# Windowed attention and a mixture of experts on eight cores: two software-pipelined steps of the attention loop are issued further behind their producer

## The chip, the cores and the metric

The kernel runs as one program on all 8 cores of a Trainium2 chip (two dies of four cores). Each core works on its own 2048 tokens and no core waits for another. The metric is the device time in microseconds (us) of the slowest core.

## What is computed

One layer on x of shape (2, 8192, 1024): attention over a window of 17 positions with 16 heads of 64, then a feed-forward part with 8 experts (the best two of each token are weighted) and a shared expert. Each part is followed by a residual addition and a layer normalization. The change concerns the first part, cut to its core here:

```python
q = _ln(silu(x @ Wq).reshape(B, L, H, D), q_g, q_b)
k = _ln(kv[..., :C].reshape(B, L, H, D), k_g, k_b).reshape(B, L, C)
scores = stack([einsum('blhd,blhd->blh', q, k_pad[:, w:w + L]) for w in range(K)]) * SCALE
attn = softmax(scores - (1.0 - soft_mask) * MASK_PENALTY, axis=-1)
out = sum(attn[..., w][..., None] * v_pad[:, w:w + L] for w in range(K))
x = _layernorm(x + silu(out @ Wout))
```

## The kernel before

A core takes its tokens in two halves of 1024, one after the other. A half goes through these stages: transposing x, the projections to q, k, v; the attention loop; normalization and router; the shared expert and four pairs of experts; the last normalization.

`Prog` (from line 70) records all operations in program order and gives each engine its own, in that order. It adds semaphore waits where two operations touch the same bytes (in PSUM: the same bank). So every engine runs strictly in the order in which the Python code emits, and an instruction that waits holds back all behind it on its engine. DMAs are issued by the queue of an engine (`sync` here), and wait in that queue's order too. The helpers give the profile its line numbers: matmuls are L336 (`mm`), transposes on TensorE L342 (`tr`), activations L351 (`act`), copies on ScalarE L355 (`scopy`), VectorE's operations L363 and L364 (`vop`), DMAs L328.

The attention loop (line 716) runs over 8 tiles of 128 tokens. A round i does, in this order:

- `knorm(i + 2)` and `qnorm(i + 1)`: two VectorE operations each, from `kpark` and `qpark` into `bscr`, for k also 8 transposes and a copy into R2.
- The scores of tile i: 8 transposes of q, a VectorE operation into `qfm`, then 32 matmuls, 144 columns for each head, into the banks of `ps_A` and `ps_B`. ScalarE copies them to `swide`, and SP stores them to `scdram` in two DMAs.
- `emit_W(i - 3)` from round 3 on: the output projection. Two products of 8 matmuls of 512 columns, each followed by a tanh on ScalarE and two VectorE operations on `fscr`; both products use the same bank, `wob[i % 2]`. Then the residual addition into `xtm` on VectorE and a square with a sum on ScalarE.
- `emit_B(i - 2)` from round 2 on: attention times v. SP reads the weights of 144 columns for each head back from `awdram` into a buffer of `awideP`; 32 transposes, four copies by ScalarE, 32 matmuls of 64 columns, two copies, 8 more transposes and a last copy into `qpark`.
- `emit_A(i)`: SP gathers the 17 scores of each position out of `scdram` into `ccg`; VectorE and ScalarE compute the softmax (the exponential is ScalarE's operation on `ccg`), the result is `abfc`, and SP scatters it along the diagonals to `awdram`.

W(i) needs B(i) and B(i) needs A(i). After the loop stand the B's and W's that are left, in the order B(6), W(5), B(7), W(6), W(7), which I call the tail. Behind it stand the sums of the layer normalization (`u1st`), which need all 8 W's. `awideP` (line 614) has two buffers before the change, one in R1, which is free after the projections, and one in the first 2304 columns of `kpark`, whose k tiles 0 to 2 have been normalized by round 0.

Of the kernel before, what the change touches and what calls it, by code (L numbers as in the profile page):

```python
# [18 lines left out]
NT = 8  # L19
# [12 lines left out]
WIDE = NH * 144  # L32
# [186 lines left out]
def build_program():  # L219
# [34 lines left out]
    with contextlib.ExitStack() as st:  # L254
        def sb(name, shape, dt):
            return st.enter_context(nc.sbuf_tensor(name, shape, dt))
# [14 lines left out]
        R1 = sb("R1", [128, 9216], BF16)  # L271
# [3 lines left out]
        kpark = sb("kpark", [128, 9216], BF16)  # L275
# [37 lines left out]
        awideP = None  # L313
# [13 lines left out]
        def dma(eng, dst, src, tag=""):  # L327
            P.op(eng, lambda e, d=dst, s=src: e.dma_start(out=d, in_=s),  # L328
                 rd=[src], wr=[dst], dma=True, tag=tag)
# [24 lines left out]
        def scopy(out, in_, tag=""):  # L354
            P.op("scalar", lambda e, o=out, i=in_: e.copy(o, i),  # L355
                 rd=[in_], wr=[out], tag=tag)
# [67 lines left out]
        for half in range(_HLIM):  # L424
          try:
# [185 lines left out]
                    abfc[i % 3][:].rearrange("p (h w) -> p h w", h=NH),  # L611
                    tag=f"asc{hx}")

            awideP = [R1[:, 6144:6144 + WIDE], kpark[:, 0:WIDE]]

            wob = [ps_A[:, 1024:1536], ps_B[:, 1024:1536]]

            def emit_W(i):
                ao_fm = qpark[:, 1024 * i:1024 * (i + 1)]
                pg = wob[i % 2]  # L620
                th = fscr[i % 2]
                for gi in range(2):
                    for c in range(8):
                        mm(pg, ao_fm[:, 128 * c:128 * c + 128],
                           WOUT[:, 1024 * c + 512 * gi:1024 * c + 512 * gi + 512],
                           c == 0, c == 7, tag=f"wo{hx}")
                    act(th[:, 512 * gi:512 * gi + 512], pg, AF.Tanh, scale=0.5,
                        tag=f"woth{hx}")
                    vop("tensor_scalar", th[:, 512 * gi:512 * gi + 512],
                        [th[:, 512 * gi:512 * gi + 512], 0.5, 0.5],  # L630
                        (ALU.mult, ALU.add), tag=f"wosg{hx}")
                    vop("tensor_tensor", th[:, 512 * gi:512 * gi + 512],
                        [th[:, 512 * gi:512 * gi + 512], pg], (ALU.mult,),
                        tag=f"wosl{hx}")
                xsl = xtm[:, 1024 * i:1024 * (i + 1)]
                vop("scalar_tensor_tensor", xsl, [th[:], 1.0, xsl],
                    (ALU.bypass, ALU.add), accum=u1st[:, i:i + 1], tag=f"u1{hx}")
                act(qfm[0][:], xsl, AF.Square, accum=u1st[:, NT + i:NT + i + 1],
                    tag=f"u1sq{hx}")

            def emit_B(i):
                aw = awideP[i % 2]
                dma("sync", aw, aw_dram[i], tag=f"awrb{hx}")
                ao_tm = R1[:, 4096 + 1024 * (i % 2):4096 + 1024 * (i % 2) + 1024]
                for w in range(2):
                    for hh in range(8):
                        s = 8 * w + hh
                        tr(ps_t0[:, 128 * hh:128 * hh + 128],
                           aw[:, 144 * s:144 * s + 128], tag=f"aT{hx}")
                        tr(ps_t1[0:16, 128 * hh:128 * hh + 128],  # L650
                           aw[:, 144 * s + 128:144 * s + 144], tag=f"aTb{hx}")
                    scopy(ATa[w], ps_t0[:], tag=f"aTe{hx}")
                    scopy(ATb[w], ps_t1[0:16, :], tag=f"aTbe{hx}")
                    av = (ps_A[:, 0:512], ps_A[:, 512:1024])[w]
                    for hh in range(8):
                        s = 8 * w + hh
                        mm(av[:, 64 * hh:64 * hh + 64],
                           ATa[w][:, 128 * hh:128 * hh + 128],
                           R3[:, 1024 * i + 64 * s:1024 * i + 64 * s + 64],
                           True, False, tag=f"av{hx}")  # L660
                        mm(av[:, 64 * hh:64 * hh + 64],
                           ATb[w][0:16, 128 * hh:128 * hh + 128],
                           R3[0:16, 1024 * (i + 1) + 64 * s:
                              1024 * (i + 1) + 64 * s + 64],
                           False, True, tag=f"avb{hx}")
                    scopy(ao_tm[:, 512 * w:512 * w + 512], av, tag=f"aoev{hx}")
                for c in range(8):
                    tr(ps_t0[:, 128 * c:128 * c + 128],
                       ao_tm[:, 128 * c:128 * c + 128], tag=f"aoT{hx}")
                scopy(qpark[:, 1024 * i:1024 * (i + 1)], ps_t0[:],  # L670
                      tag=f"aofm{hx}")
# [44 lines left out]
            for i in range(NT):  # L716
                if i + 2 <= NT:
                    knorm(i + 2)
                if i + 1 < NT:
                    qnorm(i + 1)  # L720
                qt = bscr[i % 2]
                pst = (ps_t0, ps_t1)[i % 2]
                for c in range(8):
                    tr(pst[:, 128 * c:128 * c + 128], qt[:, 128 * c:128 * c + 128],
                       tag=f"qT{hx}")
                vop("tensor_scalar", qfm[i % 2][:], [pst[:], gq_c, qbS_c],
                    (ALU.mult, ALU.add), tag=f"qfme{hx}")

                if _S3 < 2:
                    continue  # L730
                for s in [x for x in range(NH) if x % 2 == 0] + \
                         [x for x in range(NH) if x % 2 == 1]:
                    if s < 9:
                        dst = ps_A[:, 512 * (s // 3) + 144 * (s % 3):
                                   512 * (s // 3) + 144 * (s % 3) + 144]
                    else:
                        j = s - 9
                        dst = ps_B[:, 512 * (j // 3) + 144 * (j % 3):
                                   512 * (j // 3) + 144 * (j % 3) + 144]
                    lhs = qfm[i % 2][64 * (s % 2):64 * (s % 2) + 64,  # L740
                                     128 * (s // 2):128 * (s // 2) + 128]
                    rhs = R2[64 * (s % 2):64 * (s % 2) + 64,
                             1152 * (s // 2) + 128 * i:1152 * (s // 2) + 128 * i + 144]
                    mm(dst, lhs, rhs, True, False, tag=f"sc{hx}")
                    rhsb = bmask[64 * (s % 2):64 * (s % 2) + 64,
                                 128 * i:128 * i + 144]
                    mm(dst, lhs, rhsb, False, True, tag=f"scb{hx}")
                if _S3 < 3:
                    continue
                fs_sw = swide[:].ap[0][0]  # L750
                srcA = bass.AP(ps_A[:].tensor, int(ps_A[:].offset),
                               [[1536, 128], [512, 3], [144, 3], [1, 144]])
                dstA = bass.AP(swide[:].tensor, 0, [[fs_sw, 128], [432, 3],
                                                    [144, 3], [1, 144]])
                scopy(dstA, srcA, tag=f"scevA{hx}")
                dma("sync", bass.AP(sc_dram[i].tensor, 0,
                                    [[2304, 128], [1, 1296]]),
                    swide[:, 0:1296], tag=f"scoutA{hx}")
                srcB1 = bass.AP(ps_B[:].tensor, int(ps_B[:].offset),
                                [[1536, 128], [512, 2], [144, 3], [1, 144]])  # L760
                dstB1 = bass.AP(swide[:].tensor, 1296, [[fs_sw, 128], [432, 2],
                                                        [144, 3], [1, 144]])
                scopy(dstB1, srcB1, tag=f"scevB{hx}")
                srcB2 = bass.AP(ps_B[:].tensor, int(ps_B[:].offset) + 1024,
                                [[1536, 128], [1, 144]])
                scopy(swide[:, 2160:2304], srcB2, tag=f"scevB2{hx}")
                dma("sync", bass.AP(sc_dram[i].tensor, 1296,
                                     [[2304, 128], [1, 1008]]),
                    swide[:, 1296:2304], tag=f"scoutB{hx}")
                if i >= 3:  # L770
                    emit_W(i - 3)
                if i >= 2:
                    emit_B(i - 2)
                emit_A(i)
            emit_B(NT - 2)
            emit_W(NT - 3)
            emit_B(NT - 1)
            emit_W(NT - 2)
            emit_W(NT - 1)

            ck(7)
            table(AF.Ln, AF.Exp)
# [334 lines left out]
```

How the kernel before makes its waits and increments, by code:

```python
            def _run(eng):  # L179
                for o in ops:
                    if o.eng != eng_name:
                        continue
                    need = {}
                    for d in o.deps:
                        p = ops[d]
                        pc = chan(p)
                        if not need_edge(p, o):
                            continue
                        m = p if p.inc else p.marker
                        assert m is not None, f"no marker for op {p.i} ({p.tag})"
                        v = m.cnt
                        if need.get(pc, 0) < v:
                            need[pc] = v
                    if o.dma and o.prev_target > 0:
                        if need.get(o.slot, 0) < o.prev_target:
                            need[o.slot] = o.prev_target
                    for pc in sorted(need):
                        v = need[pc]
                        if floors.get(pc, 0) >= v:
                            continue
                        eng.wait_ge(sems[pc], v)
                        floors[pc] = v
                    ins = o.emit(eng)
                    if o.inc:
                        ins.then_inc(sems[chan(o)], 16 if o.dma else 1)
                if eng_name == "sync":
                    for c in sorted(totals):
                        if c != "sync" and floors.get(c, 0) < totals[c]:
                            eng.wait_ge(sems[c], totals[c])
```

## Time and profile before

| what | value |
| --- | --- |
| time, median of 2 runs | 2311.78 us (2304.62 to 2318.95) |
| the profiled execution, its own time | 2316.63 us |
| its span, slowest core (0) | 2315.0 us |
| spans of the 8 cores | 2282.0 to 2315.0 us |
| TensorE (PE) busy, matmuls | 1564.6 us, 68% |
| VectorE (DVE) busy | 577.5 us, 25% |
| ScalarE (ACT) busy | 563.2 us, 24% |
| GpSimd (POOL) busy | 117.7 us, 5% |
| granted TensorE clock, core 0, mean | 0.773 of 2.4 GHz |

The span is the time from the first to the last instruction of a core in the profile; the profiled execution's own time lies 1.6 us above it. A row of the timeline gives the start and the duration in us, the engine, the line, the operation and its tiles (output <- input), and in brackets how long the engine had been idle and what ended that. "SPq" is SP's DMA queue, and its rows are issues and not transfers. Buffer numbers are left out in the names, so `R` stands for R1, R2 and R3 and `awdram` for all eight of its kind. The granted clock is a share of 2.4 GHz; 0.50 is 1.2 GHz.

### The profile page before, as it was taken

What the parts mean: (1) busy time and instruction counts of PE and PEld (TensorE: products, weight loads), DVE (VectorE), ACT (ScalarE), POOL (GpSimd) and SP (SyncE); (2) the same over time, 40 slices, a digit from 0 to 9 for tenths busy, and PEclk for the clock granted to TensorE, in tenths of its full rate; (3) what the DMA queues carried; (4) which work ended last, traced back from release to release, by engine and by line L of the source; (5) the groups of instructions that cost most, each with busy time, mean ns of one, the idle gap of its engine ahead of it and who ended that gap; (6) DMA issues with size and microseconds to landing.
All of it is one profiled execution on the core that took longest, in us unless ns stands there. A gap on an engine that the chain in (4) does not pass through costs nothing.

```text
span 2315.0 us, 22914 instructions; the slowest of 8 cores (2282.0 to 2315.0 us)
## 1 busy us (share of the span) xinstructions
PE 1564.6 (68%) x8368; PEld 793.4 (34%) x8492; DVE 577.5 (25%) x878; ACT 563.2 (24%) x834; POOL 117.7 (5%) x136
## 2 busy tenths in 40 slices
PE   0594255656466989889816932556564779899895
PEld 0342133323333434344403422333324334344442
DVE  0154222211311222212212542222113122212223
ACT  0353132222321112021203531222223212121122
POOL 0120000000200000000001200000002000000000
PEclk9997555556588989999956965555565889999998
DMA  9222211220182525540292222121202624445203
GB/s 227 46 37 48 70 35 50 53 45 12 19 127 37 73 37 74 78 68 1 37 203 57 37 57 60 36 65 38 56 0 43 104 37 73 67 79 73 37 1 109
DMA packets 142342, 139.38 MB, mean 60 GB/s; under 512 B 73239, under 2 KB 106136, under 8 KB 142234
## 3 DMA queue, kind: packets, MB, share of 16 engines
q0 software_dynamic: 60960, 84.55, 23.6%
q1 hardware_dynamic: 76890, 36.60, 6.4%
q10 hardware_dynamic: 4384, 16.78, 2.2%
q8 instruction: 70, 1.15, 0.2%
q14 instruction: 38, 0.31, 0.0%
HBM read 189.36 MB, written 33.10 MB: 96 GB/s over the span
## 4 chain that ended last, share of the span: by engine, by line
PE 61%; DMA 15%; DVE 9%; ACT 7%; issue 6%; another core or an unknown queue 2%; SPq 0%; DVEq 0%; ACTq 0%; POOL 0%; POOLq 0%
PE ps_A L336 37%; PE ps_B L336 16%; PE ps_t L342 8%; DVE bscr L364 3%; ACT R L355 3%; DMA wpool<-Su 3%; DMA qpark<-Wd 2%; DMA wpool<-Wd 2%; DMA scdram<-swide 2%; DMA wpool<-Sd 1%; DMA wrf<-Wr 1%; DVE xtm L364 1%; DVE fscr L364 1%; DMA bscr<-x 1%
## 5 line engine op out<-in xcount | busy, mean ns | idle before, releaser
L336 PE MATMUL ps_A<-wpool,R 128*128 128x512 bf16 x2118 | 497.8, 386 | 36.6 <-DMA wpool<-Su 18.3
L342 PE MATMUL ps_t<-sb_ident,bscr 128*128 128x128 bf16 x1312 | 147.0, 264 | 340.6 <-DVE bscr L364 208.5
L355 ACT COPY R<-ps_t 128x512 bf16<-128x512 bf16 (+2 forms) x242 | 186.4, 784 | 670.6 <-PE ps_t L342 667.6
L336 PEld LDWEIGHTS ps_A<-wpool,R 128*128 128x128 bf16 x2176 | 210.9, 99 | 279.8 <-issue 53.8
L336 PE MATMUL ps_B<-wpool,R 128*128 128x512 bf16 (+1 forms) x1072 | 238.4, 368 | 41.9 <-DMA wpool<-Sd 25.9
L351 ACT ACTIVATE fscr<-ps_A 128x512 f32<-128x512 f32 x228 | 136.8, 600 | 487.6 <-PE ps_A L336 472.7
L342 PEld LDWEIGHTS ps_t<-sb_ident,bscr 128*128 128x128 bf16 x1312 | 112.8, 118 | 394.2 <-issue 361.7
L336 PE MATMUL ps_A<-qpark,R 128*128 128x512 bf16 x750 | 179.5, 383 | 3.9 <-DVE xtm L364 2.9
L336 PEld LDWEIGHTS ps_B<-wpool,R 128*128 128x128 bf16 x1088 | 101.4, 100 | 167.3 <-issue 59.5
L336 PE MATMUL ps_A<-R 128*128 128x64 bf16 (+1 forms) x512 | 86.6, 228 | 75.9 <-ACT R L355 75.9
L342 PE MATMUL ps_t<-sb_ident,R 128*128 128x128 bf16 (+1 forms) x384 | 72.1, 282 | 46.2 <-DMA R<-awdram 41.6
L336 PEld LDWEIGHTS ps_A<-qpark,R 128*128 128x128 bf16 x768 | 73.3, 99 | 84.3 <-issue 10.2
L364 DVE SCALAR_TENSOR_TENSOR bscr<-ps_B,rwall,fscr 128x512 bf16<-128x512 f32 x64 | 48.1, 751 | 198.9 <-PE ps_A L336 175.1
L364 DVE SCALAR_TENSOR_TENSOR bscr<-ps_A,rwall,fscr 128x512 bf16<-128x512 f32 x64 | 48.1, 751 | 189.2 <-PE ps_A L336 189.2
L336 PEld LDWEIGHTS ps_A<-R 128*128 128x128 bf16 (+1 forms) x512 | 52.1, 102 | 111.8 <-issue 84.1
L336 PE MATMUL ps_B<-qpark,R 128*128 128x512 bf16 x252 | 69.9, 433 | 16.1 <-DMA qpark<-Wd 15.9
L364 DVE SCALAR_TENSOR_TENSOR xtm<-ps_B,xtm 128x512 f32<-128x512 f32 x64 | 41.3, 687 | 152.9 <-PE ps_B L336 152.9
L364 DVE TENSOR_SCALAR fscr<-fscr 128x512 f32<-128x512 f32 x32 | 13.7, 427 | 253.4 <-ACT fscr L351 253.4
L336 PE MATMUL ps_B<-wpool,qpark 128*128 128x512 bf16 x122 | 48.8, 569 | 30.5 <-DVE fscr L364 22.6
L342 PEld LDWEIGHTS ps_t<-sb_ident,R 128*128 128x128 bf16 (+1 forms) x384 | 35.5, 106 | 81.0 <-issue 53.9
L364 POOL CAST bscr<-xtm 128x1024 bf16<-128x1024 f32 x16 | 18.4, 1155 | 844.5 <-DVE xtm L364 792.0
L336 PE MATMUL ps_A<-sb_validrow,sb_bkrow 1*128 1x512 f32 (+1 forms) x12 | 8.7, 825 | 77.0 <-DMA sb_validrow<-validrow 63.9
(136 smaller groups left out, 1419.8 us busy)
## 6 DMA issues: line engine op xcount, KB each, us to landing
scdram<-swide SPq DMA_DIRECT2D x16, 648.0 KB, 3.0
xtm<-x ACTq DMA_DIRECT2D x2, 4096.0 KB, 30.5
wpool<-Wkv POOLq DMA_DIRECT2D x4, 2048.0 KB, 34.1
qpark<-Wg POOLq DMA_DIRECT2D x8, 1024.0 KB, 29.2
kpark<-Wu POOLq DMA_DIRECT2D x8, 1024.0 KB, 33.8
wpool<-Wg POOLq DMA_DIRECT2D x8, 1024.0 KB, 15.5
wpool<-Wu POOLq DMA_DIRECT2D x8, 1024.0 KB, 21.1
qpark<-Wd POOLq DMA_DIRECT2D x8, 1024.0 KB, 10.1
```

The costliest lines, as they stand in the source:

```text
L336: e.matmul(d, l, r, start=s0, stop=s1),
L342: P.op("tensor", lambda e, d=dst, s=src: e.transpose(d, s, ident[:]), rd=[src, ident[:]], wr=[dst], tag=tag, strips=strips)
L351: e.activation(o, i, f, bias=b, scale=s, accum_out=a),
L355: P.op("scalar", lambda e, o=out, i=in_: e.copy(o, i), rd=[in_], wr=[out], tag=tag)
L364: return f(o, *ii, *aa)
```

## The change

`emit_B` is issued three rounds behind `emit_A` of its tile and no longer two, `emit_W` five rounds behind and no longer three, and within a round W stands ahead of B as before. `awideP` gets a third buffer, columns 2304 to 4607 of `kpark` (k tiles 2 to 4, all normalized by round 2; the buffer is first written in round 5). After the loop there are now three B's and then five W's. No operation is added or taken away.

```diff
-            awideP = [R1[:, 6144:6144 + WIDE], kpark[:, 0:WIDE]]
+            awideP = [R1[:, 6144:6144 + WIDE], kpark[:, 0:WIDE],
+                      kpark[:, WIDE:2 * WIDE]]
...
             def emit_B(i):
-                aw = awideP[i % 2]
+                aw = awideP[i % 3]
                 dma("sync", aw, aw_dram[i], tag=f"awrb{hx}")
...
+                if i >= 5:
+                    emit_W(i - 5)
                 if i >= 3:
-                    emit_W(i - 3)
-                if i >= 2:
-                    emit_B(i - 2)
+                    emit_B(i - 3)
                 emit_A(i)
-            emit_B(NT - 2)
-            emit_W(NT - 3)
-            emit_B(NT - 1)
-            emit_W(NT - 2)
-            emit_W(NT - 1)
+            for i in range(NT - 3, NT):
+                emit_B(i)
+            for i in range(NT - 5, NT):
+                emit_W(i)
```

What this moves, at three places of the first half. On ScalarE in round 2, from the last copy of the scores (`swide<-ps_B`) on; the copies `R<-ps_t` up to `qpark<-ps_t` are B(0), `ccg<-ccg` is the exponential of A(2). Before:

```order
L355 COPY swide<-ps_B 128x144
L355 COPY R<-ps_t 128x1024
L355 COPY R<-ps_t 16x1024
L355 CAST R<-ps_A 128x512
L355 COPY R<-ps_t 128x1024
L355 COPY R<-ps_t 16x1024
L355 CAST R<-ps_A 128x512
L355 COPY qpark<-ps_t 128x1024
L351 ACTIVATE ccg<-ccg 128x272
L351 ACTIVATE R<-ps_t,gb 128x8x128
```

And after, at the same place:

```order
L355 COPY swide<-ps_B 128x144
L351 ACTIVATE ccg<-ccg 128x272
L351 ACTIVATE R<-ps_t,gb 128x8x128
L355 COPY swide<-ps_A 128x1296
L355 COPY swide<-ps_B 128x864
L355 COPY swide<-ps_B 128x144
L355 COPY R<-ps_t 128x1024
```

The seven operations of B(0) have left round 2 and stand behind the scores of round 3.

On ScalarE at the end of the tail, from the last copy of B(7) to the loading of the next activation table; `fscr` x2 are the two tanh of a W, `qfm,u1st` its square. Before:

```order
L355 COPY qpark<-ps_t 128x1024
L351 ACTIVATE fscr<-ps_A 128x512 x2
L351 ACTIVATE qfm,u1st<-xtm 128x1024
L351 ACTIVATE fscr<-ps_B 128x512 x2
L351 ACTIVATE qfm,u1st<-xtm 128x1024
L385 ACT_TABLE_LOAD
```

And after:

```order
L355 COPY qpark<-ps_t 128x1024
L351 ACTIVATE fscr<-ps_B 128x512 x2
L351 ACTIVATE qfm,u1st<-xtm 128x1024
L351 ACTIVATE fscr<-ps_A 128x512 x2
L351 ACTIVATE qfm,u1st<-xtm 128x1024
L351 ACTIVATE fscr<-ps_B 128x512 x2
L351 ACTIVATE qfm,u1st<-xtm 128x1024
L351 ACTIVATE fscr<-ps_A 128x512 x2
L351 ACTIVATE qfm,u1st<-xtm 128x1024
L351 ACTIVATE fscr<-ps_B 128x512 x2
L351 ACTIVATE qfm,u1st<-xtm 128x1024
L385 ACT_TABLE_LOAD
```

Five W's follow each other where two did; W(5), which stood between B(6) and B(7), is among them, and W(3) and W(4) come out of rounds 6 and 7.

On SP's queue from the last score store (round 7) on. Before:

```order
L328 DMA scdram<-swide 128x1008
L328 DMA kpark<-awdram 128x2304
L328 DMA ccg<-scdram 128x16x17
L328 DMA awdram<-abfc 128x16x17
L328 DMA R<-awdram 128x2304
L328 DMA kpark<-awdram 128x2304
```

And after:

```order
L328 DMA scdram<-swide 128x1008
L328 DMA kpark<-awdram 128x2304
L328 DMA ccg<-scdram 128x16x17
L328 DMA awdram<-abfc 128x16x17
L328 DMA kpark<-awdram 128x2304
L328 DMA R<-awdram 128x2304
L328 DMA kpark<-awdram 128x2304
```

Behind the last scatter (`awdram<-abfc`) three reads for B's stand instead of two.

## Rows read from the trace of the kernel before

**Rows 1.** The page's chain that ended last, shares of the span.

```profile
PE 61%; DMA 15%; DVE 9%; ACT 7%; issue 6%; another core or an unknown queue 2%; SPq 0%; DVEq 0%; ACTq 0%; POOL 0%; POOLq 0%
```

**Rows 2.** Waits in 205 to 590 us: total us, times, longest.

```profile
DVE sm L364 <- ACT ccg L351: 93.5, 8, 15.4
```

**Rows 3.** Timeline of ScalarE: the exponentials of rounds 1 and 2.

```profile
264.09 0.43 ACT L351 ACTIVATE ccg<-ccg 128x272 f32<-128x272 f32 x1 [10.09 <-DVE ccg L364]
...
303.60 0.43 ACT L351 ACTIVATE ccg<-ccg 128x272 f32<-128x272 f32 x1
```

**Rows 4.** Timeline of SP's queue, first half: score stores of rounds 1 to 5.

```profile
253.11 3.48 SPq L328 DMA_DIRECT2D scdram<-swide  x2
...
277.03 3.41 SPq L328 DMA_DIRECT2D scdram<-swide  x2
...
316.55 3.48 SPq L328 DMA_DIRECT2D scdram<-swide  x2
...
357.32 3.80 SPq L328 DMA_DIRECT2D scdram<-swide  x2
...
400.47 3.77 SPq L328 DMA_DIRECT2D scdram<-swide  x2
```

**Rows 5.** The same of the second half, rounds 1 to 5.

```profile
1406.70 3.42 SPq L328 DMA_DIRECT2D scdram<-swide  x2
...
1432.83 3.39 SPq L328 DMA_DIRECT2D scdram<-swide  x2
...
1472.35 3.71 SPq L328 DMA_DIRECT2D scdram<-swide  x2
...
1513.49 3.44 SPq L328 DMA_DIRECT2D scdram<-swide  x2
...
1555.56 3.46 SPq L328 DMA_DIRECT2D scdram<-swide  x2
```

**Rows 6.** Chain in order of time: reads for B(0) and B(3).

```profile
280.70 4.41 DMA R<-awdram
...
404.39 5.81 DMA kpark<-awdram
```

**Rows 7.** Timeline of TensorE: B(6) and W(7)'s second product; second half B(6).

```profile
522.06 1.11 PE L342 MATMUL ps_t<-sb_ident,R 128*128 128x128 bf16 x5 [13.66 <-DMA R<-awdram]
...
579.56 1.01 PE L336 MATMUL ps_B<-wpool,qpark 128*128 128x512 bf16 x2 [4.82 <-DVE fscr L364]
...
1670.81 1.32 PE L342 MATMUL ps_t<-sb_ident,R 128*128 128x128 bf16 x6 [10.99 <-DMA R<-awdram]
```

**Rows 8.** Timeline of ScalarE: B(6)'s last copy, tanhs of W(5), W(6), W(7).

```profile
539.28 1.01 ACT L355 COPY qpark<-ps_t 128x1024 bf16<-128x1024 bf16 x1 [0.82 <-PE ps_t L342]
542.40 0.60 ACT L351 ACTIVATE fscr<-ps_B 128x512 f32<-128x512 f32 x1 [2.10 <-PE ps_B L336]
...
569.06 0.60 ACT L351 ACTIVATE fscr<-ps_A 128x512 f32<-128x512 f32 x1 [2.13 <-PE ps_A L336]
573.11 0.60 ACT L351 ACTIVATE fscr<-ps_A 128x512 f32<-128x512 f32 x1 [3.45 <-PE ps_A L336]
...
577.52 0.58 ACT L351 ACTIVATE fscr<-ps_B 128x512 f32<-128x512 f32 x1
583.14 0.60 ACT L351 ACTIVATE fscr<-ps_B 128x512 f32<-128x512 f32 x1 [5.05 <-PE ps_B L336]
```

**Rows 9.** Timeline of VectorE: W(7)'s residual addition, first and second half.

```profile
585.16 1.23 DVE L363 SCALAR_TENSOR_TENSOR xtm<-fscr,xtm 128x1024 f32<-128x1024 f32 x1
...
1734.80 1.23 DVE L363 SCALAR_TENSOR_TENSOR xtm<-fscr,xtm 128x1024 f32<-128x1024 f32 x1
```

**Rows 10.** Stretches: us, busy times PE, PEld, DVE, ACT, POOL; clock, DMA, GB/s.

```profile
571.00:575.00 4.00, 3.61 (x16) 1.49 (x16) 1.08 (x2) 0.60 (x1) 0.00 (x0) 1.00 0.02 4
...
580.00:583.00 3.00, 3.00 (x8) 0.85 (x6) 0.00 (x0) 0.00 (x0) 0.00 (x0) 0.53 0.00 0
```

## The prediction

> **What bounds the kernel now.** I read the chain that ended last first [rows 1]: TensorE holds 61% of it, and in the attention stage the rest is handed between engines and DMA. So I looked there, in each half from the first scores (about 225 us) to the end of the output projections (586 us), for what a round of the loop waits on. In that stretch VectorE waits 93.5 us in eight waits for ScalarE's exponential of `ccg` [rows 2]: the softmax of a round. ScalarE works in program order, and the timeline shows what stands ahead of that exponential. In round 1, where no B is issued, it starts at 264.09 and ends an idle time of 10.09 us that VectorE's `ccg` set. In round 2, after B(0), it starts at 303.60 without idle time, behind B's last copy [rows 3]. What follows it (reciprocal, `abfc`, knorm, qnorm, transposes, the next scores) is therefore late by B. A round with B costs what B costs; B is not beside other work.
>
> The length of a round is the distance between the SP queue's issues of score stores (`scdram<-swide`). First half: 253.11, 277.03, 316.55, 357.32, 400.47, so round 1 takes 23.92 (no B, no W), round 2 39.52 (B alone), round 3 40.77, round 4 43.15 (W and B) [rows 4]. Second half: 26.13, 39.52, 41.14, 42.07 [rows 5]. So B costs 13.4 to 15.6 us in a round, but a W beside it only 1.3 to 3.6: W stands ahead of B on TensorE, in the time in which B's input is still on its way. Without W that wait shows: the read of `awdram` takes 4.41 us in round 2, and 5.81 into kpark in round 5 [rows 6].
>
> **The change part by part.** The third buffer costs and frees nothing: before, a read is issued right behind the score stores (280.70 in round 2 [rows 6]), so no read waited for its buffer. SP's order in a round stays: score stores, read for B, gather, scatter. What counts is where the B's and W's now stand.
>
> Loop. B(0) leaves round 2, which becomes a round like round 1: first half 39.52 - 23.92 = 15.6 saved, second 39.52 - 26.13 = 13.4, together 29.0 [rows 4, 5]. Rounds 3 and 4 keep a B (an earlier one) and lose their W. Round 3 becomes like round 2: 40.77 - 39.52 and 41.14 - 39.52, 2.9 saved. Round 4's B reads into kpark, where I add the 5.81 - 4.41 = 1.4 of the longer landing [rows 6]: 40.92, so 2.2 and 1.2 saved, 3.4. The bounds for rounds 3 and 4 are 0 (the wait takes all that W leaves) and 9.1 (both at 39.52, no longer landing). Rounds 5 to 7 have one W and one B as before, of lower numbers but of the same banks (W(i-5) has the parity of W(i-3)), and cost the same. Loop, both halves: 29.0 + 2.9 + 3.4 = 35.3 saved.
>
> Tail. Behind the loop stood B W B W W and stands B B B W W W W W. The first B still waits for its read, which SP issues behind the last scatter: 13.66 and 10.99 us of idle TensorE [rows 7]. That doesn't change, for B(5)'s read stands behind the same scatter, and the reads for B(6) and B(7) land behind an earlier B. From the first transpose of the first B to the end of the last residual addition, before: 585.16 + 1.23 - 522.06 = 64.3 in the first half, 1734.80 + 1.23 - 1670.81 = 65.2 in the second [rows 7, 9].
>
> After, with durations of the first half. One B, from its first transpose to the end of its last copy: 539.28 + 1.01 - 522.06 = 18.2, and the next B's transposes need the bank which that copy reads, so 18.3 from B to B. Two such steps, 36.6. The third B up to the first tanh of the W behind it: 542.40 - 522.06 = 20.3 [rows 7, 8]. Then the W's. In a row they don't overlap much. Both halves of one W use one PSUM bank, and the first tanh of the next W stands on ScalarE behind the square of this one: W(6)'s first tanh is at 569.06, its second at 573.11, W(7)'s first at 577.52. That is 8.46 from W to W [rows 8]. It was W(6) at the high clock: in 571 to 575 the granted clock was 1.00 (2.4 GHz). W(7)'s second product came after 4.82 us of idle TensorE, and in 580 to 583 the clock was 0.53, mostly the low level of 1.2 GHz [rows 7, 10]. W(7)'s second tanh, at 583.14, comes 5.6 behind its first, where W(6)'s came 4.05 behind: 1.6 for the slow product [rows 8]. A W in a row thus takes 8.46 with the clock high and 8.46 + 1.6 = 10.1 with it low; both levels stand within these few us, so for the three in the middle I take the mean, 9.3. First W 8.46, three of 9.3, and the last one from its first tanh to the end of its addition 586.39 - 577.52 = 8.9. The W's: 8.5 + 27.9 + 8.9 = 45.3. Tail after: 36.6 + 20.3 + 45.3 = 102.2, that is 37.9 more in the first half and 37.0 in the second, 74.9 together.
>
> Sum: 74.9 - 35.3 = 39.6 us slower. The profiled execution took 2316.6 us (span 2315.0), so it would be 2356.2; the median of the runs is 4.8 us below that execution, so 2311.8 + 39.6 = 2351.4. What stands behind the tail (normalization, router, the FFN with its weights) moves as a whole: its first weight loads are issued on GpSimd behind casts that need the last W.
>
> Bounds of the terms: W's all at the high clock, 2 x (3 x 0.84 + 1.6) = 8.2 less; all at the low one, 2 x (3 x 0.8 + 1.6) = 8.0 more. Rounds 3 and 4: 2.8 less or 6.3 more. Altogether +29 to +54.
>
> On the clock the Trainium skill ("TensorE: Matmul & The Clock Gate", section "HAM oscillation — how this bites in real kernels") states a rule that speaks against this change: idle gaps between bursts of matmuls put the array back to half clock, so that each burst begins slow. The trace agrees for the one gap of this kind, W(7)'s of 4.82 us. By the rule all W's in a row would go slow, which is the first rival below; by the mean of the two rows the sum stays as above.
>
> **The rivals.** First, the W's in a row all run slow. Five W's with TensorE idle twice in each let the clock fall every time: 10.1 a piece, 8.0 us above the sum, 2359.4. For it: the gap and the slow product of W(7). Against: W(7)'s first product ran right behind W(6)'s second, at the high clock [rows 10], and in a row each W but the first has such a start.
> Second, they all run at the high clock: 8.2 below, 2343.2. For it W(6); against it W(7).
> Third, on the other side: the W's overlap. They alternate between two banks and two `fscr` buffers, so five in a row might run at the distance from one's second tanh to the next's first, 577.52 - 573.11 = 4.41 us [rows 8], with the first part hidden. Tail then 36.6 + 20.3 + 4 x 4.41 + 8.9 = 83.4, 19.1 and 18.2 more, 37.3 - 35.3 = +2.0: 2313.8, no slower. It decides if ScalarE can take W(7)'s first tanh before W(6)'s square. The order says no, and in the trace that tanh starts at 577.52 right behind it.
> A gain is left only if B's in a row cost much less than 18.3, or if the kpark read's wait vanished in rounds that I hold unchanged; no row speaks for it.
>
> **How the numbers follow.** Forecast 0.60, first rival 0.20, second 0.15, third 0.03, anything else 0.02. A measurement of this kernel tells about 2% from no change, 46 us here, so the line lies at 2358.0. The forecast is 6.6 us under it: of its 0.60 I give 0.08 to slower, of the first rival 0.15. Faster 0.02, within 2% 0.75, slower 0.23. Range 2335 to 2364: it takes in both clock rivals with some us of spread of the runs (2304.6 to 2319.0), and leaves out the overlap.
>
> **What would show it.** Right: score stores of rounds 2 and 3 some 24 to 26 us apart (was 39.5), rounds 3 and 4 at 39.5 to 41, rounds 5 to 7 unchanged, the idle time of 11 to 14 us before the first B of the tail still there, B's 18.3 apart, first tanhs of W's 8.5 to 10.1 apart, and the residual additions ending about 102 us behind that B's first transpose. Wrong: a tail under 90 us, a round 2 that keeps 39 us, or a read of `awdram` for which B(6) or B(7) waits.

## The result and the profile after

The changed kernel takes 2354.37 us (median of 11 runs; before 2312.19, median of 10). The ratio to the kernel before is 1.0191, with a 95% interval of 1.016 to 1.0222, so 44 us slower (37 to 51). The forecast was 2351.4 us, 39.6 us slower. A second measurement on another chip gave 1.0174 (1.013 to 1.0217), 40 us.

The execution profiled with the result was disturbed on both dies, so the rows are those of the same kernel's second profile (the run `again` below; slowest core 2367.5 us, time 2369.1, 8 cores from 2338.1 to 2367.5; the kernel before spanned 2282.0 to 2315.0). They are from its core 1.

The timeline of SP's queue, score stores of rounds 1 to 5 in the first half (start and duration in us), answers to [rows 4]:

```profile
257.62 3.50 SPq L328 DMA_DIRECT2D scdram<-swide  x2
...
281.32 3.54 SPq L328 DMA_DIRECT2D scdram<-swide  x2
...
305.16 4.35 SPq L328 DMA_DIRECT2D scdram<-swide  x2
...
345.63 3.65 SPq L328 DMA_DIRECT2D scdram<-swide  x2
...
385.32 3.47 SPq L328 DMA_DIRECT2D scdram<-swide  x2
```

Rounds 1 to 4 take 23.70, 23.84, 40.47 and 39.69 us, where they took 23.92, 39.52, 40.77 and 43.15. Round 2 has become a round like round 1, and rounds 3 and 4 cost what a B alone costs (39.52 in round 2 before).

Then the tail. TensorE waits for the read of B(5) as it waited for B(6)'s [rows 7]; ScalarE's last copies of B(5), B(6), B(7) and the tanhs of W(3) to W(5) answer to [rows 8], VectorE's last residual addition to [rows 9]:

```profile
506.39 3.46 PE L342 MATMUL ps_t<-sb_ident,kpark 128*128 128x128 bf16 x16 [14.74 <-DMA kpark<-awdram]
```

```profile
523.63 1.01 ACT L355 COPY qpark<-ps_t 128x1024 bf16<-128x1024 bf16 x1 [0.82 <-PE ps_t L342]
...
542.02 1.01 ACT L355 COPY qpark<-ps_t 128x1024 bf16<-128x1024 bf16 x1 [0.82 <-PE ps_t L342]
...
560.42 1.01 ACT L355 COPY qpark<-ps_t 128x1024 bf16<-128x1024 bf16 x1 [0.82 <-PE ps_t L342]
...
563.84 0.60 ACT L351 ACTIVATE fscr<-ps_B 128x512 f32<-128x512 f32 x1 [2.40 <-PE ps_B L336]
569.57 0.60 ACT L351 ACTIVATE fscr<-ps_B 128x512 f32<-128x512 f32 x1 [5.13 <-PE ps_B L336]
572.92 1.06 ACT L351 ACTIVATE qfm<-xtm 128x1024 bf16<-128x1024 f32 x1 [2.75 <-DVE xtm L363]
573.89 0.19 ACT L351 ACTIVATION_READ_ACCUMULATOR qfm<-xtm 128x1 f32 x1
573.98 0.58 ACT L351 ACTIVATE fscr<-ps_A 128x512 f32<-128x512 f32 x1
579.32 0.60 ACT L351 ACTIVATE fscr<-ps_A 128x512 f32<-128x512 f32 x1 [4.76 <-PE ps_A L336]
...
583.73 0.58 ACT L351 ACTIVATE fscr<-ps_B 128x512 f32<-128x512 f32 x1
```

```profile
611.84 1.23 DVE L363 SCALAR_TENSOR_TENSOR xtm<-fscr,xtm 128x1024 f32<-128x1024 f32 x1
```

B's stand 18.4 us apart (523.63, 542.02, 560.42). The tail runs from 506.39 to 613.07, 106.7 us, where 102.2 was forecast. What is longer are the W's: 563.84, 573.98, 583.73, 593.72, 603.83. They are 9.8 to 10.1 us apart and not 8.5 and 9.3. From W(4) on each first tanh follows the square and its sum directly, and each second tanh waits some 5 us for a slow product.

The clock of two neighbouring stretches of this row of W's, TensorE idle in the first and in W(5)'s second product in the other (columns as in [rows 10]):

```profile
581.40:585.40 4.00, 0.00 (x0) 0.00 (x0) 2.06 (x4) 1.63 (x3) 0.00 (x0) 1.00 0.00 0
585.60:589.20 3.60, 3.43 (x9) 1.26 (x10) 0.03 (x1) 0.00 (x0) 0.00 (x0) 0.54 0.00 0
```

The high level (1.00, 2.4 GHz) lies in the idle time, and the product gets mostly the low one (0.54, near 1.2 GHz). On this core W(6) and W(7) repeat it: 1.00 in the idle times, 0.50 and 0.52 in the second products. On all 8 cores and in both halves the second products of W(4) to W(7), 64 in all, take 2.85 to 3.57 us, and none the 1.89 of a product with the clock high throughout.

Since single cores differ, the experiments are compared by the mean over the 8 cores of each profile, read from the same rows of each core. A round is the distance between its score store and the next round's; the tail here is counted from round 7's score store to the end of the last residual addition, so it holds round 7's own B and the wait for the read. Both halves are summed, in us:

| kernel | round 1 | round 2 | round 3 | round 4 | rounds 5+6 | tail |
| --- | --- | --- | --- | --- | --- | --- |
| before | 49.8 | 80.3 | 81.7 | 84.2 | 155.8 | 209.4 |
| buf | 51.6 | 81.5 | 82.8 | 85.1 | 155.8 | 213.8 |
| again (the change) | 50.4 | 50.2 | 81.4 | 79.9 | 156.5 | 295.2 |
| w_only | 50.5 | 80.0 | 80.7 | 79.8 | 156.0 | 259.0 |
| b_only | 50.2 | 50.3 | 81.1 | 82.6 | 154.4 | 270.4 |
| late_sq | 49.8 | 49.7 | 80.7 | 80.2 | 156.4 | 270.2 |
| tail_mix | 50.6 | 50.9 | 81.3 | 79.6 | 156.4 | 282.4 |
| early_read | 49.8 | 80.4 | 82.5 | 83.9 | 155.6 | 188.0 |
| a_first | 50.5 | 72.3 | 75.0 | 74.7 | 145.4 | 188.8 |
| deep_a_first | 50.0 | 49.9 | 74.6 | 69.9 | 144.2 | 269.4 |
| lag1 | 74.1 | 73.0 | 77.6 | 73.0 | 145.1 | 136.6 |
| lag1_sq | 73.9 | 72.7 | 77.7 | 73.1 | 144.2 | 131.7 |

`before` and `buf` do the same work in the same order and show how far two profiles differ: 4.4 us in the tail, 1 to 2 in a round. Their mean is the base below: 80.9, 82.3, 84.7, 155.8, 211.6 for round 2, 3, 4, 5+6 and the tail.

### The profile page after: what moved, and what is told of

Read it like the earlier page. It is cut to its first block, busy times and chain, and to the rows that moved or that the text cites. A ratio compares the mean times of both kernels' runs of the same rounds, so it can differ in the third digit from the quotient of the medians.

```text
span 2412.7 us, 22932 instructions; the slowest of 8 cores (2339.6 to 2412.7 us)
## 1 busy us (share of the span) xinstructions
PE 1619.1 (67%) x8372; PEld 807.7 (33%) x8492; DVE 577.7 (24%) x878; ACT 563.1 (23%) x834; POOL 117.7 (5%) x136
## 4 chain that ended last, share of the span: by engine, by line
PE 60%; DMA 16%; DVE 9%; ACT 6%; issue 6%; another core or an unknown queue 2%; DVEq 0%; SPq 0%; ACTq 0%; POOL 0%; POOLq 0%
PE ps_A L336 37%; PE ps_B L336 15%; PE ps_t L342 8%; DVE bscr L364 3%; DMA wpool<-Su 2%; ACT R L355 2%; DMA scdram<-swide 2%; DMA qpark<-Wd 2%; DMA wpool<-Wd 2%; DMA wrf<-Wr 2%; DMA kpark<-awdram 1%; DVE fscr L364 1%; DMA bscr<-x 1%; DMA wpool<-Sd 1%
## 5 line engine op out<-in xcount | busy, mean ns | idle before, releaser
L336 PE MATMUL ps_A<-wpool,R 128*128 128x512 bf16 x2118 | 521.3, 399 | 35.9 <-DMA wpool<-Su 17.3
L336 PEld LDWEIGHTS ps_A<-wpool,R 128*128 128x128 bf16 x2176 | 216.5, 102 | 295.2 <-issue 120.0
L336 PE MATMUL ps_B<-wpool,R 128*128 128x512 bf16 (+1 forms) x1072 | 251.4, 383 | 39.7 <-DMA wpool<-Sd 25.4
L336 PE MATMUL ps_A<-qpark,R 128*128 128x512 bf16 x750 | 188.4, 397 | 4.0 <-DVE xtm L364 2.9
L342 PE MATMUL ps_t<-sb_ident,kpark 128*128 128x128 bf16 x320 | 67.4, 275 | 46.8 <-DMA kpark<-awdram 44.3
L364 DVE TENSOR_SCALAR fscr<-fscr 128x512 f32<-128x512 f32 x32 | 13.7, 427 | 269.4 <-ACT fscr L351 269.4
L342 PE MATMUL ps_t<-sb_ident,R 128*128 128x128 bf16 x320 | 60.3, 289 | 25.6 <-DMA R<-awdram 18.5
L336 PE MATMUL ps_A<-wpool,qpark 128*128 128x512 bf16 x122 | 46.5, 546 | 30.6 <-DVE fscr L364 26.8
L336 PE MATMUL ps_B<-wpool,qpark 128*128 128x512 bf16 x124 | 46.3, 539 | 30.7 <-DVE fscr L364 26.6
L336 PE MATMUL ps_A<-sb_validrow,sb_bkrow 1*128 1x512 f32 (+1 forms) x12 | 8.7, 825 | 82.3 <-DMA sb_validrow<-validrow 68.0
```

Source lines behind the costliest of these rows:

```text
L336: e.matmul(d, l, r, start=s0, stop=s1),
L342: P.op("tensor", lambda e, d=dst, s=src: e.transpose(d, s, ident[:]), rd=[src, ident[:]], wr=[dst], tag=tag, strips=strips)
L364: return f(o, *ii, *aa)
```

## The experiments

**The changed kernel again** (`again`), for a profile.

> The changed kernel once more, for a profile. Theory (sum of two tails against three rounds): 39.6 us over the kernel before; round 2 of the loop about 24 us long in the first half and 26 in the second, tail 102 us from the first B's first transpose to the last residual addition. Rival (the W's in a row all at the low clock): tail 106 us, 47 us over the kernel before. Rival (the W's overlap): tail 83 us, 2 us over.

1.0174 (1.013 to 1.0217), 40 us slower. Against the base the change takes 30.7 us off round 2, 0.9 off round 3 and 4.8 off round 4, and adds 83.6 to the tail: 47.9 with rounds 5+6, inside both timed intervals. The tail of core 1's first half, 106.7 us, is that of the first rival (106), while the timed loss lies nearer to the theory's. Over all cores and both halves, 64 distances between W's in a row average 9.91 us (8.46 to 10.15). The overlap is ruled out.

**The buffer alone** (`buf`): the order of before, three buffers.

```diff
-            awideP = [R1[:, 6144:6144 + WIDE], kpark[:, 0:WIDE]]
+            awideP = [R1[:, 6144:6144 + WIDE], kpark[:, 0:WIDE],
+                      kpark[:, WIDE:2 * WIDE]]
...
-                aw = awideP[i % 2]
+                aw = awideP[i % 3]
```

> Only the third buffer for the reads of awdram, order of before. Theory: no read waits for its buffer, so no change (within 3 us). Rival (the reads into the new columns of kpark land later, or meet the normalization's reads of kpark): slower by up to 1.4 us for each of the four reads that move there, 3 to 6 us.

1.0007 (0.9972 to 1.0042): no change. The buffer neither costs nor frees anything.

**The W's alone** (`w_only`):

```diff
-                if i >= 3:
-                    emit_W(i - 3)
+                if i >= 5:
+                    emit_W(i - 5)
                 if i >= 2:
                     emit_B(i - 2)
...
-            emit_B(NT - 2)
-            emit_W(NT - 3)
-            emit_B(NT - 1)
-            emit_W(NT - 2)
-            emit_W(NT - 1)
+            for i in range(NT - 2, NT):
+                emit_B(i)
+            for i in range(NT - 5, NT):
+                emit_W(i)
```

> Only the W's moved: B two rounds behind, W five, tail B B W W W W W. Theory: rounds 3 and 4 lose the W that stood in B's wait for its read and get 6 us shorter in all, the tail grows by 38 us (18.3 + 20.3 + 45.3 = 83.9 against 64.3 and 65.2), so 32 us slower than before, most of the whole loss. Rival (it is the B's that cost, since a B in a row costs what a round gained): within 5 us of before.

1.0145 (1.0106 to 1.0184), 34 us slower. Rounds 3 and 4 give 1.6 and 4.9, together the 6 expected, and the tail takes 47.4 where 38 were expected: again W's in a row (9.97 us apart on average). Most of the loss is made by the W's.

Why a round gains so little without its W can be seen on TensorE, where the B of round 3 begins (core 1, first half). In the kernel before, behind W(0):

```profile
326.50 2.77 PE L342 MATMUL ps_t<-sb_ident,kpark 128*128 128x128 bf16 x16 [1.00 <-DMA kpark<-awdram]
```

and here, where W(0) is gone:

```profile
326.07 3.46 PE L342 MATMUL ps_t<-sb_ident,kpark 128*128 128x128 bf16 x16 [8.68 <-DMA kpark<-awdram]
```

B starts at nearly the same time. The W had filled the wait for B's read, and without it TensorE stands idle there for 8.68 us.

**The B's alone** (`b_only`), each W one round behind its B as before:

```diff
-                if i >= 3:
-                    emit_W(i - 3)
-                if i >= 2:
-                    emit_B(i - 2)
+                if i >= 4:
+                    emit_W(i - 4)
+                if i >= 3:
+                    emit_B(i - 3)
                 emit_A(i)
+            emit_B(NT - 3)
+            emit_W(NT - 4)
             emit_B(NT - 2)
```

> B three rounds behind, W four (one behind B as before), two buffers, tail B W B W B W W. Theory: round 2 gives back 29.0 us and round 3 2.9 in both halves together; the tail grows by one B and one W between B's, 26.6 us in each half (from B(6)'s last copy to B(7)'s in the kernel before), 53.3; so 21 us slower than before. Rival (a B costs the same in the loop and behind it and the W's that go with it are free): within 5 us of before.

1.0071 (1.0039 to 1.0104), 16 us slower (21 expected). Round 2 gives 30.6, and the tail grows by 58.8 (53.3 expected). A B moved out of the loop together with a W is no gain either.

**The squares later** (`late_sq`, `late_sq2`): the changed kernel, with each W's square in the tail issued behind the next W's first tanh.

```diff
                     act(th[:, 512 * gi:512 * gi + 512], pg, AF.Tanh, scale=0.5,
                         tag=f"woth{hx}")
+                    if late and gi == 0 and i > NT - 5:
+                        sq_W(i - 1)
...
-                act(qfm[0][:], xsl, AF.Square, accum=u1st[:, NT + i:NT + i + 1],
-                    tag=f"u1sq{hx}")
+                if not late or i == NT - 1:
+                    sq_W(i)
```

> The changed kernel, with the square of each W in the tail issued behind the first tanh of the next W. Theory (ScalarE's order sets 4.41 us of the distance between two W's in a row, the slow product 5.7): the next first tanh starts when its product is done, some 3.5 us behind the second tanh at the low clock, so W's 9.2 us apart instead of 10.1 and about 7 us less than the changed kernel in the two tails together, 35 us over the kernel before. Rival (VectorE's residual addition sets the distance): W's stay at 10.1 and the time at 40 to 44 us over.

The tails are 25.0 us shorter than those of the changed kernel, more than three times the 7 expected; timed 1.0125 (1.0031 to 1.022). The timeline of ScalarE, core 1, W(4)'s second tanh, then both of W(5) and of W(6):

```profile
576.93 0.60 ACT L351 ACTIVATE fscr<-ps_B 128x512 f32<-128x512 f32 x1 [1.13 <-PE ps_B L336]
...
581.72 0.60 ACT L351 ACTIVATE fscr<-ps_B 128x512 f32<-128x512 f32 x1 [2.02 <-PE ps_B L336]
583.45 0.60 ACT L351 ACTIVATE fscr<-ps_A 128x512 f32<-128x512 f32 x1 [1.13 <-PE ps_A L336]
...
588.24 0.60 ACT L351 ACTIVATE fscr<-ps_A 128x512 f32<-128x512 f32 x1 [2.02 <-PE ps_A L336]
589.97 0.60 ACT L351 ACTIVATE fscr<-ps_B 128x512 f32<-128x512 f32 x1 [1.13 <-PE ps_B L336]
```

Here the first tanh of the next W comes 1.73 us behind the second of this one (581.72 to 583.45), not 4.41, and the second 4.79 behind the first, so W's stand 6.52 apart. The stretch behind these rows (same columns):

```profile
576.00:590.00 14.00, 8.06 (x36) 3.17 (x34) 7.61 (x14) 4.72 (x9) 0.00 (x0) 1.00 0.00 1
```

The clock is high throughout this stretch. TensorE's timeline shows how long it stood idle ahead of a second product, in this kernel

```profile
579.74 1.89 PE L336 MATMUL ps_B<-wpool,qpark 128*128 128x512 bf16 x8 [2.90 <-ACT qfm L351]
...
586.26 1.89 PE L336 MATMUL ps_A<-wpool,qpark 128*128 128x512 bf16 x8 [2.91 <-ACT qfm L351]
...
592.77 3.19 PE L336 MATMUL ps_B<-wpool,qpark 128*128 128x512 bf16 x8 [2.90 <-ACT qfm L351]
```

and in the changed one:

```profile
585.77 3.44 PE L336 MATMUL ps_B<-wpool,qpark 128*128 128x512 bf16 x8 [4.83 <-DVE fscr L364]
```

The earlier tanh was forecast; that with it the idle time falls from 4.8 to 2.9 us, and that most second products then run fast, was not in the expectation. Not all do: the third row, W(7)'s, has the same idle time ahead of it and is slow. Of the 64 second products of W(4) to W(7) on all cores 40 take 1.89 us here and 24 over 3 us, where none took less than 2.85 in the changed kernel. Over all cores the distance between W's is 7.00 us (5.77 to 8.46). That the shorter idle time is what keeps the clock high is likely but not shown, since no run changes it by itself. A second run of the same kernel (`late_sq2`) shows whether the time agrees:

> late_sq once more, since its first timing had an interval of 1.0 to 2.2% over before while the tails in its profile were 25 us shorter than those of the changed kernel. Theory: 18 us over the kernel before (43 - 25), W's in a row 6.5 us apart with a second product at the high clock. Rival (7 us less than the changed kernel, as expected at first, and the clock rose by chance): 35 us over, W's 9.2 apart on most cores.

1.0102 (1.0063 to 1.0141), 24 us over the kernel before: some 18 us less than the change, and the rival's 35 lies outside. On cores 4 to 7 of its profile W's stand 7.16 us apart on average (5.78 to 8.70): nearer to the 6.5 of the theory than to the rival's 9.2, with some second products still slow.

**Another order in the tail** (`tail_mix`): the changed kernel's loop, and behind it

```diff
             for i in range(NT - 3, NT):
                 emit_B(i)
-            for i in range(NT - 5, NT):
+                emit_W(i - 2)
+            for i in range(NT - 2, NT):
                 emit_W(i)
```

> The loop of the changed kernel, tail B W B W B W W W. Theory: a W between two B's costs 26.6 - 18.3 = 8.3 us instead of 10.1 in a row, for its sums run beside B's transposes, and three W's stand so: 5 us less in each half, 10 in all, 32 to 34 us over the kernel before. Rival (order in the tail is no matter, only how many B's and W's stand there): 40 to 44 us over.

The tails are 12.8 us shorter than those of the changed kernel (10 expected). The timing, 1.0188 (1.014 to 1.0236), doesn't show it; an interval of 22 us can't tell 10. So the profile speaks for it and the time leaves it open.

**B(6)'s read ahead of the last scatter** (`early_read`), in the kernel before; `load_B` is the read split off `emit_B`:

```diff
                 if i >= 2:
+                    load_B(i - 2)
                     emit_B(i - 2)
+                if i == NT - 1:
+                    load_B(NT - 2)
                 emit_A(i)
```

> The kernel before, with the read of awdram for B(6) issued ahead of emit_A(7) instead of behind its scatter. Theory (the 11 to 14 us of idle TensorE ahead of the tail are the SP queue's order: the read stands behind a scatter that waits for the exponential behind B(5)): the wait goes, 13.7 + 11.0 = 25 us faster than before. Rival (B(6)'s data themselves are late, or the wait moves to B(7), whose read needs the last scatter): less than 10 us.

0.9929 (0.9892 to 0.9966), 16 us faster (8 to 25), and the tail is 23.6 shorter. The idle time ahead of the tail was SP's order. The lag of B can't remove it, since the read stands behind that scatter at any lag, as the 14.74 us of the changed kernel show.

**A ahead of B** (`a_first`), in the kernel before:

```diff
                 if i >= 2:
-                    emit_B(i - 2)
+                    load_B(i - 2)
                 emit_A(i)
+                if i >= 2:
+                    emit_B(i - 2)
```

> The kernel before, with emit_A(i) ahead of B(i-2), and only the read for B(i-2) issued ahead of it. Theory (B stands in series because the exponential, and with it knorm and qnorm, is queued behind B's copies on ScalarE): VectorE's part is done beside B, so the 5.5 us between B's end and the next transposes go in rounds 2 to 5, some 2 in round 6, and the last scatter comes before B(5) ends, so the 11 to 14 us ahead of the tail go too: 35 us in each half, 70 in all. Rival (rounds are set by TensorE's own sequence of B, transposes and scores): only the tail's wait goes, 25 us.

0.9773 (0.974 to 0.9806), 53 us faster. Rounds 2 to 6 are 36.3 us shorter in all and the tails 22.8. So a part of B did stand in series because of the exponential behind it, and the rival's 25 us are passed. Less came than the 70 forecast: each of rounds 2 to 4 gives some 4.3 us and not 5.5. The timeline of ScalarE in round 2, from the copies of the scores on, shows one reason:

```profile
294.93 1.07 ACT L355 COPY swide<-ps_B 128x864 f32<-128x864 f32 x2
307.67 0.43 ACT L351 ACTIVATE ccg<-ccg 128x272 f32<-128x272 f32 x1 [11.68 <-DVE ccg L364]
308.01 1.89 ACT L355 COPY R<-ps_t 128x1024 bf16<-128x1024 bf16 x2
```

Now B's first copy waits for the exponential: it starts 13.1 us behind the last copies' start (294.93), where it took 11.7 in the kernel before (276.85 to 288.59 on its core 0).

The larger part of B stays in series even so: round 2 takes 72.3 us where round 1 takes 50.5, so a B still adds 21.8 us in both halves, where it added 30.5 in `before` (80.3 against 49.8). TensorE's timeline at the end of this B(0) shows what holds them, the transposes for knorm (`bscr`):

```profile
321.41 0.58 PE L342 MATMUL ps_t<-sb_ident,R 128*128 128x128 bf16 x4 [0.28 <-ACT R L355]
321.79 1.06 PE L342 MATMUL ps_t<-sb_ident,bscr 128*128 128x128 bf16 x8
```

They follow B's last transposes without idle time, though VectorE had finished their input, and qnorm's, by 314.5. Ahead of this B TensorE had stood idle for 8.44 us for its read. So once the exponential is out of the way the rival's mechanism, TensorE's own order of B, transposes and scores with the wait for B's read in it, sets the length of the round.

**The change on top of A first** (`deep_a_first`): the lags 3 and 5 of the change and its third buffer, with A ahead of B.

> The changed kernel with emit_A(i) ahead of B(i-3), only B's read ahead of it, as in a_first. Theory (a moved B or W costs what it takes in a row behind the loop less what it took in its round): with A first a round hides more of B (round 2 cost 35.6 and 36.7 us against 24 and 26 without B), so the change costs more on top of a_first than on top of the kernel before: tails 84 us longer, rounds 2 to 4 27 us shorter, 57 us over a_first, 5 us over the kernel before. Rival (it was the serial exponential that made the change lose, so without it the lag is no matter): within 10 us of a_first.

Its timing gave no interval (4 runs, 2303.0 the lowest, and 2299.2 the lowest of before beside it). By the profiles it is 51.8 us over a_first: 22.4 off round 2, 0.4 off round 3, 4.8 off round 4, 1.2 off rounds 5+6, and 80.6 on the tail. That is the 57 expected within the spread of profiles and far from the rival's 10. Round 2 gives back only 22.4 where it gave 30.7, since it had hidden more of its B. In the sum the lag costs 51.8 against 47.9 on the kernel before, which two profiles can't tell apart. The loss isn't tied to the serial exponential.

**The lags shortened** (`lag1`), on top of A first: B(i-1) and W(i-2) in round i. The edit, against the kernel before:

```diff
-                if i >= 3:
-                    emit_W(i - 3)
                 if i >= 2:
-                    emit_B(i - 2)
+                    emit_W(i - 2)
+                if i >= 1:
+                    load_B(i - 1)
                 emit_A(i)
-            emit_B(NT - 2)
-            emit_W(NT - 3)
+                if i >= 1:
+                    emit_B(i - 1)
+            load_B(NT - 1)
             emit_B(NT - 1)
             emit_W(NT - 2)
```

> The change's direction turned round, on top of a_first: B(i-1) and W(i-2) in round i, tail B W W. Theory: the tail loses a B with a W beside it, 26.6 us in each half, round 1 gains a B, 12, round 2 a W, 2: 12 us less in each half, 25 us under a_first, 75 to 80 under the kernel before. Rival (B one round behind its softmax waits for the scatter and the read, in each round or in the tail): no faster than a_first.

0.9647 (0.9612 to 0.9681), 82 us faster than before. Round 1 grows by 23.6 and the tail shrinks by 52.2 against a_first; with the other rounds 27.3 less (25 expected). B one round behind its softmax waits for nothing new: on core 1 the wait for round 1's read, 8.46 us, is like that of round 2 in a_first (8.44), and the transposes of the last B start 1.25 us behind those of the B ahead of it, having waited for a copy of ScalarE and for no read.

**Both** (`lag1_sq`): `lag1` with the late square of `late_sq` for W(6).

> lag1 with W(6)'s square behind W(7)'s first tanh. Theory: 1.7 to 2 us less in each tail, 2 to 4 us under lag1, which only the tails in the profile can tell.

0.9606 (0.9569 to 0.9644), 91 us faster than the kernel before, with a median of 2218.68 us. The tails are 4.9 us shorter than lag1's (2 to 4 expected), about the spread of two profiles; W(7) stands 7.46 us behind W(6) in all 16 of them, where it is 9.75 on average in lag1. It beats both kernels, and TensorE is as busy as ever; the page of its slowest core:

```profile
span 2216.8 us, 23042 instructions; the slowest of 8 cores (2190.2 to 2216.8 us)
## 1 busy us (share of the span) xinstructions
PE 1578.3 (71%) x8492; PEld 793.8 (36%) x8492; DVE 577.2 (26%) x878; ACT 563.7 (25%) x834; POOL 117.7 (5%) x136
```

## Why the prediction was right

The time (2354.4 against 2351.4), the sign and the size (44 and 40 us against 39.6) came out as forecast, by the mechanism forecast, with one term too small. Step by step, both halves:

- Third buffer at nothing: right, 1.0007.
- Round 2 gives back a B, 29.0: 30.7 in the profiles.
- Rounds 3 and 4 lose the W that stood in the read's wait, 2.9 + 3.4 = 6.3: 0.9 + 4.8 = 5.7. The sum is right, and by the mechanism told: without the W TensorE is idle for 8.84 us ahead of round 4's B, as it is in w_only. The split is not. w_only, late_sq and tail_mix agree with the change that round 3 gives 0.9 to 1.6 and round 4 gives 4.5 to 5.1. The forecast read 2.9 for round 3 from core 0, where the mean of the cores of the base has 1.4 between rounds 2 and 3; and the 1.4 us for a longer landing in `kpark`, which it added to round 4, doesn't show: round 4 of the change reads into `kpark` and takes 79.9, round 2 before reads into R1 and takes 80.9. The two errors cancel, which is luck.
- Rounds with a W and a B unchanged, first read of the tail unchanged: right (155.8 and 156.5 for rounds 5+6; 14.74 us of wait, 14.31 on the same core before).
- B to B 18.3: right, 18.4.
- W's in a row at 8.46 and then 9.3: too small. They take 9.91 on average, because the low clock of the second product is the rule and the high one the exception. For the four distances of a tail that is 39.6 instead of 36.4, 6.5 us in both halves. This is most of the 8.7 us by which the tail's 83.6 exceed the forecast 74.9; the other 2.2 are within the spread. The first rival, which I gave 0.20, had the W's right; the sum with it, 47.6, is what the profiles add up to (47.9), while the timed 44 and 40 lie between both. That the time came out nearer to 39.6 is no merit of this term, which is too small in every profile. The Trainium skill's rule on idle gaps ("TensorE: Matmul & The Clock Gate", section "HAM oscillation — how this bites in real kernels") was the better guide than the mean of two rows: by it every burst behind an idle gap begins slow, and all 64 second products were slow, wholly or for the most part. late_sq shows its other side only in part: with 2.9 us of idle time in place of 4.8 most of them ran fast, and 24 of 64 did not.
- The overlap of W's didn't come, as ScalarE's order said. late_sq shows that this order was indeed what stood against it: with the square moved, the next tanh follows 1.7 us behind.
- That a round is longer by the whole of its B because ScalarE's exponential stands behind it: right as a price, and in part as a reason. With the exponential ahead of B (a_first) rounds 2 to 4 lose some 4.3 us each, and the rest of B stays in series by TensorE's own order. The sum rested on the price alone, so it isn't touched.

What stays open: the profiles of 8 cores add up to 48 us and the timings to 40 and 44, with intervals of 15 to 20 us. I can't say whether the few us between are real.

## What to carry to other kernels

Issuing a consumer further behind its producer pays only if it waited for that producer. Here only the last read waited for `awdram` being written (7.2 us on SP's queue, once, in the first half of core 0); what looked like a dependency was an in-order queue (an exponential behind B's copies, a read behind a scatter). Reordering within the round removed the wait ahead of the tail and some 4 us of each B. Each further stage of lag moves work from rounds, where something else covers part of it, behind the loop, where less does: compare the cost of one more piece in the tail with what its round becomes without it, and take the shortest lag at which nothing waits.

## What the runs showed of the hardware

The granted clock can fall into the wrong phase of a repeated sequence. In the changed kernel, on core 1, TensorE was idle for 4.83 us ahead of the second products of W(5), W(6) and W(7); the clock was 1.00 in the idle stretches and 0.50 to 0.54 in the products. With the idle times cut to 2.9 us, by an operation moved on ScalarE, it stayed at 1.00 for 14 us, and 40 of 64 second products took 1.89 us instead of 2.85 to 3.57; the other 24 still took over 3. An edit that should have given 7 us gave 25 in the profiled tails and some 18 by the time.
